# Query, key and value products moved from a block after each round into the units of the round after next

## What is computed

```
x = x + L0_conv(ln_c(x))
t = t + L0_ffn(ln_t(t))          # per image: two of eight experts, D=128, F=256,
                                 # then a layer norm with gamma and beta
x = x + L1_conv(ln_c(x))         # begins with qkv = w_qkv applied to each pixel (3 x 128 outputs)
t = t + L1_ffn(ln_t(t))
```

## Time and profile before

| | |
|---|---|
| median of 3 runs | 3741.39 us (3738.98 to 3753.02) |
| the profiled execution | 3733.62 us, its span 3731.8 us |
| PE busy | 3180.7 us (85%) |
| DVE, ACT, POOL busy | 1662.4, 1523.1, 811.6 us |
| first matmul of a unit in ffn0 | at 696.24 us |
| last product matmul of ffn0 | issued at 1473.38 us |

### The profile page before, as it was taken

The page is one execution under the profiler, slowest core; times in us unless marked ns, Lnnn a source line. Parts: engine busy times, 40 slices in busy tenths (PEclk is TensorE's granted clock), DMA queues, the critical chain, the costliest instruction groups (busy, mean ns, idle before and its releaser), DMA issues. The chain is left out here.

```text
span 3731.8 us, 66873 instructions
## 1 busy us (share of the span) xinstructions
PE 3180.7 (85%) x27136; PEld 1709.0 (46%) x27136; DVE 1662.4 (45%) x2331; ACT 1523.1 (41%) x2263; POOL 811.6 (22%) x694
## 2 busy tenths in 40 slices
PE   5656575598989995999995669999999999999999
PEld 1146322344444552565664244646454554546444
DVE  5723265465555533111111344545464554545453
ACT  3311243266666663112122244535354444445433
POOL 2410242133333443111110102121211112121221
PEclk8768665799999996999998799999999999999999
DMA  5321464323333324777776231313223131313000
GB/s 187 147 74 23 160 237 181 139 83 131 127 128 130 140 110 159 193 216 207 215 197 187 78 119 51 109 67 102 80 76 106 46 102 57 119 46 124 12 12 23
DMA packets 192537, 438.59 MB, mean 118 GB/s; under 512 B 33340, under 2 KB 100156, under 8 KB 183740
## 3 DMA queue, kind: packets, MB, share of 16 engines
q1 hardware_dynamic: 192356, 436.20, 35.0%
HBM read 247.40 MB, written 188.75 MB: 117 GB/s over the span
## 5 line engine op out<-in xcount | busy, mean ns | idle before, releaser
L2088 DVE TENSOR_TENSOR d_scaled<-d_hid,d_ps 128x512 f32<-128x512 f32 x512 | 331.4, 684 | 604.6 <-PE d_ps L1788 553.3
L1777 PE MATMUL d_ps<-d_scaled,d_w 128*128 128x512 f32 x1024 | 527.8, 597 | 1.3 <-DVE d_scaled L2088 1.3
L1956 ACT ACTIVATE d_hid<-d_ps,d_b 128x512 f32<-128x512 f32 x512 | 350.3, 687 | 381.2 <-PE d_ps L1768 374.5
L1519 PE MATMUL c_ps<-c_pad,c_weight 32*32 32x512 f32 x13824 | 473.8, 600 | 25.7 <-ACT c_pad L1471 18.8
L1519 PEld LDWEIGHTS c_ps<-c_pad,c_weight 32*32 32x32 f32 x13824 | 286.6, 103 | 212.4 <-issue 128.8
L1766 PE MATMUL d_ps<-d_tnh,d_w1h 128*128 128x512 f32 x512 | 295.4, 577 | 9.2 <-ACT d_hid L1956 9.2
L1135 PE MATMUL b_ps<-b_hid,b_w2s 128*128 128x512 f32 x512 | 272.6, 618 | 13.0 <-ACT b_hid L1204 7.2
L1204 ACT ACTIVATE b_hid<-b_ps,b_w1s 128x512 f32<-128x512 f32 x256 | 174.1, 687 | 205.4 <-PE b_ps L1128 203.6
L2038 POOL CAST d_tnh<-d_TN 128x512 fp32r<-128x512 f32 x64 | 40.4, 631 | 989.2 <-PE d_ps L1768 966.6
L1777 PEld LDWEIGHTS d_ps<-d_scaled,d_w 128*128 128x128 f32 x1024 | 195.6, 191 | 44.8 <-DVE d_scaled L2088 2.7
L1580 DVE COPY c_pad<-c_P 128x1024 f32<-128x1024 f32 x48 | 33.4, 696 | 404.6 <-PE c_ps L1519 377.4
(11 more groups left out here) (265 smaller groups left out, 5787.0 us busy)
## 6 DMA issues: line engine op xcount, KB each, us to landing
scratch_qkv<-b_qkv SPq DMA_DIRECT2D x64, 768.0 KB, 3.5
c_P<-scratch_qkv SPq DMA_DIRECT2D x192, 256.0 KB, 4.7
scratch_agg<-c_out SPq DMA_DIRECT2D x192, 256.0 KB, 4.9
d_buf<-scratch_qkv SPq DMA_DIRECT2D x96, 512.0 KB, 4.1
d_buf<-scratch_agg SPq DMA_DIRECT2D x96, 512.0 KB, 3.6
p_X<-in_x SPq DMA_DIRECT2D x8, 2048.0 KB, 7.7
scratch_s<-p_X SPq DMA_DIRECT2D x8, 2048.0 KB, 6.3
m_X<-scratch_s SPq DMA_DIRECT2D x8, 2048.0 KB, 7.6
```

The costliest lines, as they stand in the source:

```text
L1519: end = nc.tensor.matmul(ps[on(i), k * QUADS + h, :].rearrange("p (b r w) -> p b r w", b=2, w=HB), weight[k][on(q), 2 * r + x, on(h)], pad ...
L1777: nc.tensor.matmul(moe_bank, w2[:, e, :], scaled[n % 3][:, :], start=False, stop=(e == E - 1)).then_inc(moe_pe, 1)
L1956: nc.scalar.activation(hid[n % 3][:, :], hid_bank(n), ACT.Gelu, bias=b1[:, n % E:n % E + 1]).then_inc(hid_done, 1)
L2088: nc.vector.tensor_tensor(scaled[n % 3][:, :], hid[n % 3][:, :], spread_bank(n), ALU.mult).then_inc(scaled_done, 1)
```

## The change

The phase becomes B + 2 rounds of 32 units. In round s every engine does, unit by unit, what belongs to image s (hidden layer), then the norms of image s - 1, and then, in units 3 to 26, one product of image s - 2. Round 0 has the units alone, round 1 units and norms, round 8 norms and products, round 9 products alone. The block of 24 products after a round is gone. `variances` of the first norm moves from the block's end to unit 2, the casts of the first norm from units 5 to 8 to units 6 to 9, and `invert` is issued in two halves. To give the products PSUM banks beside the units', the hidden tiles get two banks (3, 4) where they had three, the chunk's sum gets one (6) where it had two, and the products get two (5, 7). So `down` of a new chunk waits for the `add` of the chunk just before it. SP's stores and loads are put in the order in which their data now come.

The core of the diff:

```diff
-        hid_bank = lambda n: banks[3 + n % 3][:, :]
-        y_bank = lambda c: banks[6 + c % 2][:, :]
-        qkv_bank = lambda j: banks[3 + j][:, :]
+        hid_bank = lambda n: banks[3 + n % 2][:, :]
+        y_bank = banks[6][:, :]
+        qkv_bank = lambda m: banks[5 + m % 2 * 2][:, :]
+        QKV = 3
+        product_at = lambda u: divmod(u - QKV, 3) if QKV <= u < QKV + 3 * NCH else None
...
-                    pe.wait_ge(hid_done, n + 1)
+                    pe.wait_ge(hid_done, n + 2)
...
-                        pe.wait_ge(z_done, b * NCH + c + 1)
+                        pe.wait_ge(z_done, b * NCH + c + 2)
...
-                    for j in range(3):
-                        pe.wait_ge(copied, n * 3 + j + 1)
+                    pe.wait_ge(copied, m + 2)
...
+                for s in range(B + 2):
+                    for u in range(UNITS):
+                        if s < B:
+                            unit(s, u)
+                        if 0 <= s - 1 < B:
+                            norms(s - 1, u)
+                        if s >= 2 and product_at(u):
+                            product(s - 2, *product_at(u))
+                    if s < B:
+                        down(s, UNITS - 2)
+                        down(s, UNITS - 1)
...
+                        if s < B:
+                            gelu(s, u)
+                        if 0 <= s - 1 < B:
+                            norms(s - 1, u)
+                        if s < B and 25 <= u < 31:
+                            sum_squares(s, u - 25)
+                        if s >= 2 and product_at(u):
+                            copy(s - 2, *product_at(u))
...
+                        if s < B and 4 <= u < 28 and u % UPS == 0:
+                            split(s, u // UPS + 1)
+                        if s >= 2 and u % 3 == 1 and u < 3 * NCH:
+                            rest(s - 2, u // 3)
+                        if 0 <= s - 1 < B and 8 <= u < 12:
+                            for c in pair(u - 8):
+                                add(s - 1, c)
...
+                        if s < B and u >= 6 and u % UPS == 2:
+                            add(s, u // UPS - 1)
+                        if 0 <= s - 1 < B:
+                            norms(s - 1, u)
+                        if s >= 2 and u % 3 == 0 and u < 3 * NCH:
+                            high(s - 2, u // 3)
+                        if s + 1 < B and 9 <= u < 16:
+                            choose(s + 1, u - 9)
+                        if s + 1 < B and u == 23:
+                            choose(s + 1, E - 1)
```

More of the change, by code:

```diff
@@ new lines, in norms @@
+                def norms(b, u):
+                    if u == 2:
+                        norm.variances(pe, 2 * b)
+                    if 6 <= u < 10:
+                        for c in pair(u - 6):
+                            norm.cast_inverse(pe, 2 * b, c, sum_free(b))
+                    if u == 15:
+                        norm.means(pe, b, x(b), lambda c: pe.wait_ge(x2_done, b * NCH + c + 1))
+                    if 18 <= u < 22:
+                        for c in pair(u - 18):
+                            norm.cast_mean(pe, b, c, mean_free(b))
+                    if u == 23:
+                        norm.variances(pe, 2 * b + 1)
+                    if 28 <= u < 32:
+                        for c in pair(u - 28):
+                            norm.cast_inverse(pe, 2 * b + 1, c, image_free(b))
@@ new lines, in copy, with norms @@
+                def copy(b, c, j):
+                    m = (b * NCH + c) * 3 + j
+                    if j == 0:
+                        act.wait_ge(qkv_stored[c % 2], (b * (NCH // 2) + c // 2) * 16 + 16)
+                    act.wait_ge(qkv_pe, m + 7)
+                    nc.scalar.activation(qkv[c % 2][:, j, :], qkv_bank(m), ACT.Copy).then_inc(copied, 1)
+                def norms(b, u):
+                    if u < 2:
+                        sum_squares(b, 6 + u)
+                    if u == 2:
+                        norm.deviations(act, 2 * b, eps_t)
+                    if u == 4:
+                        norm.split(act, 2 * b, 1)
+                    if 7 <= u < 11:
+                        for c in pair(u - 7):
+                            norm.wait_out(act, 2 * b, c)
+                            nc.scalar.activation(tn(b)(c), tn(b)(c), ACT.Identity, bias=gb[:, 1:2], scale=gb[:, 0:1]).then_inc(affine_done, 1)
+                    if u == 16:
+                        norm.split(act, b, 0)
+                    if 19 <= u < 23:
+                        for c in pair(u - 19):
+                            norm.squares(act, 2 * b + 1, c, tn(b), lambda c: norm.wait_centred(act, b, c))
+                    if u == 24:
+                        norm.deviations(act, 2 * b + 1, eps_c)
+                    if u == 27:
+                        norm.split(act, 2 * b + 1, 1)
@@ L1269, in _ @@
[L1269 to L1292 removed]
+                    pool.wait_ge(affine_done, b * NCH + c + 1)
@@ new lines, in add, with rest @@
+                    nc.gpsimd.tensor_tensor(x(b)(c), x(b)(c), tn(b)(c), ALU.add).then_inc(x2_done, 1)
+                def rest(b, c):
+                    pool.wait_ge(xh_done, b * NCH + c + 1)
+                    pool.wait_ge(qkv_pe, (b * NCH + c) * 3 + 3)
+                    nc.gpsimd.tensor_tensor(xl[c % 2][:, :], tn(b)(c), xh[c % 2][:, :].bitcast(F32), ALU.subtract).then_inc(xl_done, 1)
+                split(0, 0)
+                split(0, 1)
+                for s in range(B + 2):
+                    for u in range(UNITS):
[6 more added lines that the diff above has]
+                                add(s - 1, c)
+                        if s + 1 < B and u in (28, 31):
+                            split(s + 1, (u - 28) // 3)
@@ new lines, in _ @@
+                for s in range(B + 2):
+                    for u in range(UNITS):
+                        if s < B and u >= 6 and u % UPS == 2:
[8 more added lines that the diff above has]
+                            choose(s + 1, E - 1)
+                    if s < B:
+                        add(s, NCH - 1)
```

198 lines of the change are left out of this document (48 added, 150 removed).

## The result

The changed kernel takes 3755.85 us (median of 5 runs, 3749.03 to 3758.35) against 3739.1 us for the kernel before in the same series: a ratio of 1.0041, 95% interval 1.0022 to 1.0059. So it is slower by 0.4%, 17 us, where 3765 us and +24.7 us were forecast. The profiled execution took 3750.29 us, its span 3748.5 us.

A forecast was written before the change was run, and what follows sets the result against it. PE was taken as the bound: a full round of 80.4 us work, 14.0 waits and 3.4 clock makes 97.8 against 95.1; the stage sums to 802.2 against 777.5, +24.7 us, forecast 3765 us, 8-in-10 range 3716 to 3797.

The forecast's parts named there:

- PE's own work at full clock: A full round's units, casts, `means` and `variances`, and products on PE with nothing waiting: 80.4 us.
- unit 10 behind `scale`, `high`, `choose`: PE's `down` waits for an `add` that DVE reaches 6.9 us after the casts, against 1.4 of work: 5.5 us.
- unit 14: DVE takes 11.4 us plus 0.4 between adds with four experts, PE has 9.0 of work: wait 2.8 us.
- unit 26 behind the reciprocal, and unit 28: `add` behind the second norm's reciprocal: 8.4 us against PE's 5.9, wait 2.5, and 0.3 at unit 28's casts.
- slow clock: Loss to PE's granted clock in a full round: 3.4 us, near the 3.8 before; ends 0 and 6.
- the bar that the prediction set: The main step is wrong if PE's waits for `add` come to less than 8 us a round.
- Two hidden banks at nothing: `up` waits for the Gelu of the last unit but one; taken as no cost, bounds 0 to 1.4 us a round.
- Rounds 8 and 9: Stage's end without units: 54 us for norms with products partly in their gaps, then 26.5 us.
- `choose` did not get shorter: Faster rival, chance 0.24: POOL is through more adds, DVE's `choose` runs at 0.40 us an instruction, total 3716 us.
- The no-change case: Rival, chance 0.18: waits of units 10, 14 and 26 and slow clock overlap, 14 us a round, total 3742 us.
- the copies held up none that mattered: Much slower rival, chance 0.10: ACT's copies waiting for stores delay Gelus and PE, +36 us, total 3800 us.
- The harder rule of the Trainium skill: DVE and GpSimd lock a shared port for whole instructions; each `rest` costs DVE up to 1.3 us, 6 over the stage.

The follow-up runs named there:

- both edits: Changed kernel with two banks for the chunk's sum, three for the last 48 products, and `choose` at units 14 to 23: 3661.77 us, 0.9806 of before.

## Why the prediction was right, and where its sizes were off

The direction and the mechanism were right: the block's waits go, the one sum bank's come, and they come to about the same. The forecast was +24.7 us; the medians give +16.8, and the stage +15.4. That the whole came as near as this is in part luck: of the stage's 802.2 us the rounds 2 to 6 were put 13.2 us too long (489.0 against 475.8), and rounds 1 and 9 2.2 and 2.4 too long, while rounds 0 and 8 were put 4.6 and 4.0 too short. By its own steps, for a full round (round 2 of after):

| term | predicted us | measured us |
|---|---|---|
| PE's own work at full clock | 80.4 | 81.5 |
| unit 10 behind `scale`, `high`, `choose` | 5.5 | 4.93 |
| unit 14 | 2.8 | 0.93 |
| unit 22 | 1.2 | 0.77 |
| unit 26 behind the reciprocal, and unit 28 | 2.8 | 2.52 |
| unit 30, and the joined parts | 1.7 | 1.21 |
| slow clock | 3.4 | 2.6 |
| sum | 97.8 | 94.5 |

The first line's measured value is the round of 83.08 us with both edits (983.12 to 1066.20), less its 1.63 us of waits (0.59, 0.23, 0.50 and 0.31). The 2.52 are 2.22 us at unit 26 and 0.30 at the casts of unit 28. The clock's is PE's busy time in 843.57 to 937.92, 83.86, less the 81.21 of a round at full clock. The round itself took 94.35 us. Its clock is the best of the five: in their mean PE was busy 84.93 us, so the clock took 3.7, close to the 3.4 predicted, and a round 95.2.

- *Unit 14* is the term that was mis-sized. DVE's side was right: 11.8 us from `add` to `add` predicted, and 872.98 to 884.75 measured, 11.77. PE's side was not: it was priced at full clock, 9.0 us. PE's `down`s between the one at 873.77 and the one at 885.56 (shown above):

```profile
877.67 1.02 PE L1148 MATMUL b_ps<-b_hid,b_w2s 128*128 128x512 f32 x2
...
879.94 1.02 PE L1148 MATMUL b_ps<-b_hid,b_w2s 128*128 128x512 f32 x2
```

  The unit behind the long wait takes 3.90 us at a granted clock of 0.58, the next 2.27 at 1.00. PE needed 10.86 us (885.56 less 873.77, less the wait of 0.93) and not 9.0, and unit 14 waited that much less. The prediction had this as a doubt worth 1 us over the whole, and counted the clock and the wait in full beside each other; it is 1.9 us in round 2 and more in the other four, where unit 14 waited 0.34 to 0.70 us. That DVE's side came out at 11.8 is partly luck: three of the experts' instructions were lengthened beside POOL between the two `add`s (0.83, 1.48 and, at 880.82, 1.51 us; 2.4 us over 0.48 each), where it was six in before (4.0 us), but the `high` at 879.51 waited 1.13 us for PE and took 0.99, where 0.4 in all had been put.
- *Waits for `add`* passed the bar that the prediction set (8 us a round): 10.06. Rounds of 94.35 to 96.4 us are above its other bar, 94, but three of the five are below the 96 to 100 that it named. The waits at unit 14 and 26 were to be 2 to 3 us; unit 14's was under 1.
- *Two hidden banks at nothing* held in the rounds: the third bank gives 0.5 us at most (0 to 1.4 were the bounds). Not in round 0, which took 61.0 us against 56.4 predicted and 57.4 with three hidden banks. There PE waited 0.83 us for a Gelu, then 2.32 us at unit 14 (1.2 predicted), with a mean clock of 0.90. In the kernel with `choose` on 16 columns, whose round 0 is that of after, it took 61.1. With three hidden banks unit 14 waited as long (2.33 us), but PE was idle 0.8 us less in all and busy 2.8 us less, at a clock of 0.95. Other kernels with two hidden banks had 0.91 and 0.92 there, so how much of the 2.8 us the bank causes stays open.
- *Round 1*: 87.3 predicted, 85.1 measured, by two errors that cancel in part: PE was idle 14.25 us and not 20.2, and busy 70.82 where work and clock had been put at 67.1. *Round 7*: 89.0, 88.9. *Rounds 8 and 9*: 54.0 and 26.5 predicted, 58.0 and 24.1 measured, 82.1 together against 80.5. Round 8 has 11 us more than the norms alone had (46.7), so, less the 2 us that the prediction allowed for its later first `variances`, more than half of its 16.8 us of products was not hidden. The prediction's 54 stood 7.3 us above the lower of its bounds, 46.7 and 65.5, and 2 us under their middle; the measured 58.0 is 2 us over it.
- *The rivals*: `choose` did not get shorter (1.35 us beside POOL, four of POOL's adds after its `rest`), for the reason that the prediction gave. The no-change case was half true in its mechanism: the slow clock did fall into unit 14's wait. None of PE's idle stretches in round 2 ended on a Gelu, so the copies held up none that mattered.
- *The harder rule of the Trainium skill* ("SBUF — State Buffer", section "Who interferes with whom") agrees with the traces better than the 0.9 us a POOL instruction taken from the rows: with 16 columns a `choose` instruction went from 0.23 to 1.31 us, 1.1 us lost to each of POOL's. The `rest` among the experts (from 880.58) did cost one of them 1.03 us (1.51 against 0.48). The 6 us that this adds up to over the stage don't show in the sum, since fewer of the other instructions met POOL than in before, as told above.

Where the change's gain went: with the sum's second bank, and three banks for the last products, the products in the rounds would have been worth 57 us (3738.5 less 3681.4); giving them that bank cost 74 us (3755.85 less 3681.39, of which rounds 8 and 9 are 82.1 - 80.2 = 1.9).

## What to carry to other kernels

Before work is moved in between other work, count the buffers of both together: a second accumulator between an engine that works in order and the engine that empties it bought four units of slack here, and the overlap of the products was worth less than that. Give the scarce banks by stretch, not for the whole phase: one bank for products beside units was enough; where nothing stands between them, 24 products took 56.3 us with one bank, 24.1 with two and 21.4 with three. And when two waits follow each other with a slow clock between, price them together: the second wait shrank here by what the clock cost the engine that waits, 1.9 of 2.8 us.

## What the runs showed of the hardware

- A `choose` instruction on DVE that ran beside one of GpSimd's tensor instructions ended just behind it, whether it worked on 16 columns (0.03 to 0.05 us behind) or on 257 and 258 (0.11 to 0.15 us, in the first expert), and those that started with it took 1.24 to 1.36 us; alone they took 0.23 and 0.35 to 0.48 us. DVE's `add`, which reads a PSUM bank, kept its 0.74 us beside them (872.98 and, with 16 columns, 872.46).
- Products that wait for a copy between one another kept the granted clock at 0.50 for 56 us, in two kernels. PE was idle 0.78 to 0.84 us ahead of each product there. With three banks, where its idle stretches for ACT were 0.27 to 0.32 us, the same round had 0.89.
- The clock behind a wait: behind each wait of 4.9 us in rounds 2 to 6 of after PE ran slow (0.58 over 3.90 us in round 2, 0.50 over 3.9 to 4.0 us in the other four). Behind the waits of 2.2 us at unit 26 it did so in some rounds (0.57 from 1112.15, 0.56 from 1208.30) and not in others (1.00 from 922.79 and from 1304.28); two sum banks had a wait of 2.12 us in a round at 1.00. With no wait over 0.6 us the clock was 1.00 in both full rounds shown.
